# Graph attention and graph convolution on one core: four second-layer tiles a batch in halves by casting DMAs, the bias added by an accumulating DMA

## What is computed

```python
# first layer, per batch
h = input @ W;  f1 = h @ a1;  f2 = h @ a2
e = f1 + swapaxes(f2, 1, 2);  e = where(e >= 0, e, 0.2 * e)
attention = softmax(adj * e, axis=1)
x = attention @ h + bias + input
# second layer
support = x @ W1 + b
y = adj @ support
y = (y - mean) * rsqrt(var + 1e-5) * gamma + beta      # over batches and nodes
return relu(y) + x
```

## Time and profile before

| | |
|---|---|
| median of 3 runs | 909.66 us (909.13 to 911.93) |
| profiled execution | 911.96 us, its span 910.2 us |
| PE busy | 871.0 us, 96% |
| ACT busy | 804.2 us, 88% |
| DVE busy | 726.1 us, 80% |
| POOL busy | 211.6 us, 23% |
| moved by DMA | 246.39 MB, queue busy 71.7% |
| granted PE clock | 0.984 of full speed over the span, 1.00 in the batches |

### The profile page before, as it was taken

How to read it: one execution, slowest core, us unless ns; L and a number is a source line. 1 busy time by engine, 2 the same in 40 slices (tenths; PEclk the granted TensorE clock), 3 DMA queues, 4 the chain that set the end, 5 groups by cost and what they waited for, 6 DMA issues and landing times.

```text
span 910.2 us, 8919 instructions
## 1 busy us (share of the span) xinstructions
PE 871.0 (96%) x3167; PEld 547.5 (60%) x3167; DVE 726.1 (80%) x794; ACT 804.2 (88%) x614; POOL 211.6 (23%) x166
## 2 busy tenths in 40 slices
PE   6999999999999999999999999999999999999960
PEld 4335556675656756676566756567566765666850
DVE  3655788797878888887877978788888978879966
ACT  5998699988999799998999889997999979997645
POOL 0012214250333112341142401341113411323000
PEclk9999999999999999999999999999999999999995
DMA  8996676748677595867767495775957677565988
GB/s 337 422 362 240 260 291 237 292 165 334 224 273 268 203 360 173 294 234 267 280 237 300 155 357 207 267 274 199 358 174 292 231 263 287 192 224 190 423 335 344
DMA packets 46220, 246.39 MB, mean 271 GB/s; under 512 B 5560, under 2 KB 6184, under 8 KB 19552
## 3 DMA queue, kind: packets, MB, share of 16 engines
q1 hardware_dynamic: 46176, 245.82, 71.7%
HBM read 221.57 MB, written 24.23 MB: 270 GB/s over the span
## 4 chain that ended last, share of the span: by engine, by line
PE 83%; DVE 7%; ACT 3%; issue 2%; DMA 2%; SPq 1%; POOL 0%; DVEq 0%; ACTq 0%; POOLq 0%
PE acc L526 40%; PE acc L499 10%; PE acc L493 10%; PE acc L495 10%; DVE exp_lo L765 4%; PE acc L480 4%; PE acc L507 2%; PE acc L454 2%; PE acc L539 1%; PE acc L542 1%; PE acc L541 1%; ACT scores L623 1%; DMA adj_slot<-biasT 1%; DVE stats L786 1%; ACT hi L637 1%
## 5 line engine op out<-in xcount | busy, mean ns | idle before, releaser
L746 DVE CUSTOM_DVE_ANT_0 scores<-scores,adj_slot 128x2048 f32<-128x2048 f32 x128 | 297.5, 2324 | 77.5 <-ACT scores L616 30.2
L765 DVE SCALAR_TENSOR_TENSOR exp_lo<-scores,rz,hi 128x2048 fp32r<-128x2048 f32 (+1 forms) x133 | 280.5, 2125 | 0.0
L616 ACT ACTIVATE scores<-adj_slot,f_cols 128x2048 f32<-128x2048 f32 x128 | 255.0, 1998 | 15.4 <-PE acc L499 11.8
L623 ACT ACTIVATE scores<-scores,neg_mx 128x2048 f32<-128x2048 f32 x128 | 255.1, 1993 | 14.2 <-DVE neg_mx L749 14.2
L637 ACT ACTIVATE hi<-scores,rz 128x2048 fp32r<-128x2048 f32 (+1 forms) x133 | 227.5, 1726 | 33.6 <-DVE rz L758 30.4
L526 PE MATMUL acc<-adj_slot,region_even 128*128 128x512 f32 x512 | 228.8, 592 | 0.0
L526 PE MATMUL acc<-adj_slot,region_odd 128*128 128x512 f32 x392 | 175.3, 592 | 0.8 <-DVE region_odd L801 0.8
L526 PEld LDWEIGHTS acc<-adj_slot,region_even 128*128 128x128 f32 x512 | 96.7, 190 | 99.7 <-issue 95.7
L499 PE MATMUL acc<-exp_lo,h_hi 128*128 128x512 f32 x448 | 121.5, 391 | 0.8 <-DVE exp_lo L765 0.7
L526 PEld LDWEIGHTS acc<-adj_slot,region_odd 128*128 128x128 f32 x392 | 74.0, 190 | 77.2 <-issue 73.2
L495 PE MATMUL acc<-hi,h_hi 128*128 128x512 f32 x448 | 119.9, 390 | 0.0
(11 more groups left out here) (77 smaller groups left out, 614.7 us busy)
## 6 DMA issues: line engine op xcount, KB each, us to landing
adj_slot<-adjT SPq DMA_DIRECT2D x159, 1024.0 KB, 5.1
adj_slot<-xT SPq DMA_DIRECT2D x20, 1024.0 KB, 7.6
adj_slot<-biasT SPq DMA_DIRECT2D x32, 256.0 KB, 6.5
xp_dram<-adj_slot SPq DMA_DIRECT2D x32, 256.0 KB, 2.6
adj_slot<-xp_dram SPq DMA_DIRECT2D x8, 1024.0 KB, 12.1
adj_slot<-f_rows SPq DMA_DIRECT2D x7, 1024.0 KB, 6.9
adj_slot<-y_dram SPq DMA_DIRECT2D x7, 1024.0 KB, 12.0
outT<-adj_slot SPq DMA_DIRECT2D x6, 1024.0 KB, 4.7
```

What stands on the lines that cost most here:

```text
L616: act.activation(scores[t % ER][:, :], slots[f1_slot(bt.par)][:, :], ACT.Prelu, bias=f2_cols[:, bt.n, t:t + 1], alpha=ALPHA).then_inc(edge ...
L623: act.activation(scores[e][:, :], scores[e][:, :], ACT.Exp, bias=neg_mx[:, e:e + 1], accum_out=zsum[:, e:e + 1]).then_inc(exp_done, 1)
L746: dve.tensor_tensor_reduce(scores[e][:, :], scores[e][:, :], slots[s][:, :], 1.0, NEG_BIG, ALU.mult, ALU.max, mx[:, e:e + 1]).then_inc(max ...
L765: dve.scalar_tensor_tensor(exp_lo[e][:, part_cols(t, i)], scores[e][:, part_cols(t, i)], rz[:, e:e + 1], hi[m][:, part_cols(t, i)].bitcast ...
```

## The change

Three things change.

- **Halves for four tiles.** Places 3, 7, 10 and 14 of the second layer (tiles 5, 9, 12 and 0) are taken in halves, in batches 1 to 6; in batch 0 only places 10 and 14 (`FIRST_HI`). The hi half of the tile is loaded from DRAM once more by a DMA on POOL's queue whose destination is float32r, so that it rounds (`load_hi`), into a slot that is lent for it (`HI_AT`: the spare slot of tile 8, those of tiles 2 and 3, and that of tile 9). DVE makes the lo half in place (`tile_low`), in steps 1, 5, 8 and 11 (`LOW_STEP`). POOL splits the 128 columns of support that go with it (`split_support`), into one small buffer `part_hi`. PE takes 12 matmuls (`layer1_halves`).
- **The bias.** x is loaded a place earlier, and a DMA on POOL's queue adds the bias, reading biasT and accumulating into the slot of x. Its semaphore counts whole, so `make_xp` waits for all of it. Slot 9 no longer holds the bias.
- **Slots in turns.** In odd batches tiles 2, 3, 4 and tiles 9, 11, 10 swap slots (`SWAP`). The next batch's tiles 2, 3 and 4 are loaded at the end of the step before (`load_early`), around the store of x'. The adj tiles of lent slots are loaded again behind places 3 to 6 (`RELOAD`), into the slot that the second layer has left; tiles 2 and 3, lent now as well, behind places 7 and 10 (`LENT`), for the next step.

```diff
-    T_F, T_BIAS, T_X, T_RES = 8, 9, 10, 11
+    T_F, T_HI, T_X, T_RES = 8, 9, 10, 11
+    SWAP = {2: T_HI, 3: T_RES, 4: T_X}
+    SWAP.update({late: early for early, late in SWAP.items()})
+    HI_AT = {3: T_F, 7: 2, 10: 3, 14: T_HI}
+    LOW_STEP = {3: 1, 7: 5, 10: 8, 14: 11}
+    RELOAD = {T_F: 3, T_HI: 4, T_X: 5, T_RES: 6}
+    FIRST_HI = [10, 14]
+    LENT = {u: max(k for k in HI_AT if HI_AT[k] == u) for u in HI_AT.values() if u not in (T_F, T_HI)}
...
# SP
+            def load_early(nx, t):
+                wait_lent(nx.prev(), SWAP[t])
+                load_adj(nx, t)
+
+            def load_again(bt, t):
+                if t == T_F:
+                    sp.wait_ge(edge_out, NT * (bt.n + 1))
+                elif t in LENT:
+                    wait_l1(sp, bt.prev(), LENT[t])
+                elif not is_last(bt):
+                    wait_l1(sp, bt, SIGMA.index(SWAP[t]))
+                else:
+                    wait_lent(bt, t)
...
                     for k, t in enumerate(SIGMA):
                         wait_l1(sp, pv, k)
-                        if t >= PRE:
+                        if t >= PRE and k > 2:
                             load_adj(bt, t)
-                        elif not is_last(bt):
+                        elif t < PRE and not is_last(bt):
                             load_adj(nx, t)
-                        if k == 1:
-                            load_again(pv, T_F)
-                        if k == 2:
-                            load_again(pv, T_BIAS)
-                        if k == 3:
-                            load_again(pv, T_X)
+                        for t in RELOAD:
+                            if RELOAD[t] == k:
+                                load_again(pv, t)
+                        for t in LENT:
+                            if LENT[t] == k:
+                                load_again(bt, t)
-                        if k == T_BIAS + 1:
-                            load_bias(bt)
+                        if k == T_RES + 1:
+                            load_residual(bt)
-                        if k == 4:
-                            load_again(pv, T_RES)
-                        if k == T_RES + 2:
-                            load_residual(bt)
...
+                if not is_last(bt):
+                    load_early(nx, 2)
+                    load_early(nx, 3)
                 store_xp(bt)
+                if not is_last(bt):
+                    load_early(nx, 4)
...
# PE
+            def layer1_halves(bt, k):
+                t = SIGMA[k]
+                tile_hi = slots_lo[hi_slot(bt, k)]
+                pe.wait_ge(part_lo_done, split_no(bt, k))
+                pe.wait_ge(hi_loaded[k], hi_value(bt, k))
+                for c in range(NC):
+                    pe.matmul(acc1[c][:, :], part_lo[bt.par][:, tile_cols(t)], tile_hi[:, cols(c)], start=False, stop=False)
+                for c in range(NC):
+                    pe.matmul(acc1[c][:, :], part_hi[:, :], tile_hi[:, cols(c)], start=False, stop=False)
+                pe.wait_ge(tile_lo_done, split_no(bt, k))
+                for c in range(NC):
+                    mm = pe.matmul(acc1[c][:, :], part_hi[:, :], slots_lo[l1_slot(bt, t)][:, cols(c)],
+                                   start=False, stop=False)
+                mm.then_inc(l1_tile, 1)
...
# DVE
+                dve.wait_ge(hi_loaded[k], hi_value(bt, k))
+                dve.tensor_tensor(slots_lo[l1_slot(bt, t)][:, :], slots[l1_slot(bt, t)][:, :],
+                                  slots_lo[hi_slot(bt, k)][:, :].bitcast(F32), ALU.subtract).then_inc(tile_lo_done, 1)
...
-                dve.wait_ge(xb_done, NC * bt.n + c + 1)
+                dve.wait_ge(xb_done, 16 * (bt.n + 1))
...
+                    for k in (() if is_first(bt) else halved(bt.n - 1)):
+                        if LOW_STEP[k] == t:
+                            tile_low(bt.prev(), k)
...
# POOL
+            def load_hi(bt, k):
+                nx = bt.next()
+                if HI_AT[k] == T_F:
+                    pool.wait_ge(edge_out, NT * (bt.n + 1))
+                else:
+                    pool.wait_ge(max_done, NT * nx.n + HI_AT[k] + 1)
...
+                pool.dma_start(slots_lo[hi_slot(bt, k)][:, :], adjT[bt.n, tile_cols(SIGMA[k]), :])\
+                    .then_inc(hi_loaded[k], 16)
...
-            def add_bias(bt, c):
+            def add_bias(bt):
                 pool.wait_ge(res_loaded, 16 * (bt.n + 1))
-                pool.wait_ge(bias_loaded[c], 16 * (bt.n + 1))
-                pool.tensor_tensor(res_sb[:, cols(c)], res_sb[:, cols(c)], bias_sb[:, cols(c)], ALU.add)\
-                    .then_inc(xb_done, 1)
+                pool.dma_start(res_of(bt)[:, :], biasT, accum_op=ALU.add).then_inc(xb_done, 16)
...
-                    for b in range(NB):
-                        split_h(bt, b)
-                for c in range(NC):
-                    add_bias(bt, c)
+                    pv = bt.prev()
+                    split_h(bt, 0)
+                    halves_of(pv, 3, split_support)
+                    split_h(bt, 1)
+                    halves_of(pv, 7, load_hi)
+                    split_h(bt, 2)
+                    halves_of(pv, 10, load_hi)
+                    halves_of(pv, 7, split_support)
...
+                add_bias(bt)
+                if not is_last(bt):
+                    halves_of(bt, 3, load_hi)
```

More of the change, by code:

```diff
@@ L166, in build @@
         xn_loaded = sem("xn_loaded")
[L167 to L168 removed]
+        again_loaded = {t: sem(f"again_loaded{t}") for t in (T_F, T_HI, T_X, T_RES, *LENT)}
+        hi_loaded = {k: sem(f"hi_loaded{k}") for k in HI_AT}
+        part_hi_done, part_lo_done = sem("part_hi_done"), sem("part_lo_done")
+        tile_lo_done = sem("tile_lo_done")
         res_loaded = sem("res_loaded")
@@ L205, in adj_value, with again_value, hi_slot, split_no @@
                 return 16 * (bt.half + 1)
-            return 16 * (bt.n + 1 + (t in STAGED))
+            return 16 * (bt.n + 1 + (slot_of(bt.par, t) in STAGED))
         def l1_slot(bt, t):
-            if t == T_F and not is_last(bt):
+            if t in (T_F, T_HI, T_RES, T_X) and not is_last(bt):
                 return slot_of(1 - bt.par, t)
             return slot_of(bt.par, t)
+        def again_value(bt, t):
+            return 16 * (bt.n + (t not in LENT))
+        def hi_slot(bt, k):
+            if HI_AT[k] == T_F:
+                return l1_slot(bt, T_F)
+            return slot_of(1 - bt.par, HI_AT[k])
+        def split_no(bt, k):
+            return sum(len(halved(n)) for n in range(bt.n)) + halved(bt.n).index(k) + 1
+        def halved(n):
+            return FIRST_HI if n == 0 else list(HI_AT)
+        def hi_value(bt, k):
+            return 16 * (bt.n + (k in FIRST_HI))
         def part_cols(t, i):
@@ L561, in step @@
                         while ahead < min(t + (LEAD if t > 0 else LEAD - 1), NT):
-                            layer1(bt.prev(), ahead)
+                            if ahead in halved(bt.n - 1):
+                                layer1_halves(bt.prev(), ahead)
+                            else:
+                                layer1(bt.prev(), ahead)
                             ahead += 1
@@ L572, in step @@
                     for c in range(NC):
-                        make_h(nx, x1_sb if is_first(bt) else xn_sb, acc1, c)
+                        make_h(nx, x1_sb if is_first(bt) else xp_of(bt), acc1, c)
                 for c in range(NC):
@@ L642, in adj_high @@
                 t = SIGMA[LAST_SPLIT[m]]
-                if t in (T_BIAS, T_X, T_RES):
-                    act.wait_ge(again_loaded[t], 16 * (bt.n + 1))
+                if t in again_loaded and t != T_F:
+                    act.wait_ge(again_loaded[t], again_value(bt, t))
                 else:
@@ L758, in recip, with tile_low @@
                 dve.reciprocal(rz[:, e:e + 1], zsum[:, e:e + 1]).then_inc(rz_done, 1)
+            def tile_low(bt, k):
+                t = SIGMA[k]
+                if t in again_loaded and (bt.n > 0 or t not in LENT):
+                    dve.wait_ge(again_loaded[t], again_value(bt, t))
+                else:
+                    dve.wait_ge(slot_loaded[slot_of(bt.par, t)], adj_value(bt, t))
+                dve.wait_ge(hi_loaded[k], hi_value(bt, k))
+                dve.tensor_tensor(slots_lo[l1_slot(bt, t)][:, :], slots[l1_slot(bt, t)][:, :],
+                                  slots_lo[hi_slot(bt, k)][:, :].bitcast(F32), ALU.subtract).then_inc(tile_lo_done, 1)
             def exp_low(bt, t):
```

76 lines of the change are left out of this document (53 added, 23 removed).

## The result

The changed kernel takes 901.53 us (median of 6 runs, 901.14 to 905.20). The kernel before, measured beside it, takes 910.76 (909.13 to 911.95). The ratio is 0.9908 with a 95% interval of 0.9888 to 0.9928, so the change gives 9.2 us. 892.9 was predicted: the sign is right and the time is in the stated range (to 908), but only about half of the forecast gain of 16.8 came.

The account below looks back on a forecast made before the run. PE's matmuls were taken to bound the kernel, except at batch ends, where an ACT and DVE loop is as long. -17.9 + 1.4 - 2.3 + 2.0 = -16.8 us, from 909.66 to 892.9; range 888.5 to 908.

Parts of the forecast that it names:

- Halves, -17.9: Second layer on PE: 26 tiles taken in halves at 2.74 us instead of 3.43, saving 0.69 us each, -17.9 us.
- DVE, +1.4: DVE's added subtractions, 2.28 us each, delay scores and reciprocals; PE waits 0.2 us a batch, +1.4 us.
- Tail relief, -2.3: Batch ends: without POOL's bias additions two exp_lo run faster and the tail's 0.5 us wait goes in five batches, -2.3 us.
- Batch 0, +2.0: Batch 0: the accumulating DMA takes 7.5 us, so the bias sum is in at 92; +2.0 us, between -0.8 and +5.5.
- The step that failed: Batch end: x staged a tile sooner lands near 387, the sum is wanted near 403, leaving the bias DMA about 16 us.
- the sign of being wrong: Stated test of the forecast: it is wrong if PE waits over 1 us a batch or a casting load costs over 3.8 us.
- Their delay matters little: DMA queues: delay of the casting and accumulating transfers matters little, since a casting load goes out 20 to 35 us before use.
- B: Rival, chance 0.20: at batch ends ACT and DVE lag PE or collisions stay; PE waits 8.1 us in all, 901.
- C: Rival, chance 0.16: DMA queues bind, delaying tile loads and scores; decides from 3.8 us per special transfer; 925 at 4.25 us.
- D: Rival, chance 0.07: tile 9 lands too late for DVE in step 5; 2.5 us in each of seven batches, 910.
- The early loads: Next batch's tiles 2, 3 and 4 loaded early: no gain by itself, but puts ACT up with PE, covering the subtractions.
- the lower end that I took: DMA queues: a casting or accumulating transfer costs 2.83 us, like a plain one; the upper end was some 5.1 us.

## Why the prediction was right or wrong

**The sum, term by term.** The kernel with the residual x behind tile 15 differs from the changed kernel in one number, so it measures the terms without the lost batch ends. From the chains, in us from the span's start:

| kernel | second layer of batch 0 starts | first make_h after it | sixth make_h | span |
|---|---|---|---|---|
| before | 94.88 | 194.19 | 724.57 | 910.2 |
| bias alone | 98.53 | 197.19 | 726.12 | 911.2 |
| changed | 95.70 | 195.35 | 717.01 | 899.2 |
| x behind tile 15 | 96.58 | 193.80 | 708.27 | 890.5 |

- *Halves, -17.9.* Right. Steady batches with PE always busy last 105.78 without halves (the bias alone) and 102.90 with four: 2.88, or 0.72 a tile where 0.69 was forecast. 26 of them are 18.7 us.
- *DVE, +1.4.* Too much: PE waits for nothing in these batches. The subtraction takes 2.59 us on average in the changed kernel, where 2.3 was forecast, and DVE's 96 us of a batch still fitted. They fitted narrowly, as the run with 2.27 us more on DVE shows.
- *Tail relief, -2.3.* Right. In the kernel with the bias alone the steps of the table are shorter than before by 0.65, 1.45 and 0.55, together 2.65, and the two exp_lo take 4.6 where 4.7 was forecast. (Five batches at 0.5 would have been 2.5; 2.3 is two thirds of seven.)
- *Batch 0, +2.0.* +0.8 in the changed kernel, +1.7 and +3.65 in the two others, all inside the stated range. The accumulating DMA takes 8.34 us there, where 7.5 was taken. The transfers were thought of and the granted clock wasn't: where PE stood for 1.99 to 3.03 us, 1.6 us of the loss are the clock's. In the changed kernel PE happened to stand only 1.25. From trace to trace this start moves by up to 4.7 us with the same code, so one trace doesn't size the term.

-18.7 - 2.65 + 1.7 make -19.65, and the span with x behind is 890.5 against 910.2, -19.7. So the terms that were named hold; the missing 8.7 us (899.2 against 890.5) are one that wasn't. That the 892.26 of this kernel stands so near the forecast 892.9 is luck in part: its gain is 19.7 us and not 16.8, and the forecast was counted from 909.66, where the kernel before took 911.99 beside it.

**The step that failed** is on the bias: "x is staged a tile sooner and lands near 387 on that clock, and the sum isn't wanted until the first layer is over, near 403: the DMA has about 16 us. It gives something at the tail." The move of x was taken as room for the bias, and only the transfer that was moved was priced; what it does to tile 15 was put at nothing, without a reason. I did not ask what stands behind it on SP's queue, and that is tile 15, the one load at whose end everything waits. What it cost stands in the table: against the kernel with x behind, the changed one loses 2.4 us in the first step (99.65 against 97.22), 7.2 in the next five (521.66 against 514.47) and nothing in the last, and has 0.9 less in batch 0. That is 1.6 us a batch in six batches, over the 1 us that the forecast itself named as the sign of being wrong.

It shows as well in "Their delay matters little: a casting load goes out 20 to 35 us ahead of its use". It is true of the casting loads (their median is 5.5 us to landing and nobody waits), and it was the wrong transfer to look at: what a fuller queue delays is also every plain load, and the one of tile 15 has 5.2 us from its issue to the start of its score in the kernel before (385.32 to 390.5) and in the changed kernel only about 1 us to spare.

**The rivals.** *B*'s number, 901, was hit by the result, but not by its mechanism: the tail did bind, through a tile load and not through ACT and DVE being late. DVE's waits over the whole span of the changed kernel have this (line waited for: us in total, times, longest):

```profile
DVE scores L815 <- DMA adj_slot<-adjT: 25.2, 17, 4.0
```

In the kernel before such waits come to 20.4 us in 28 times, the longest 2.0.

*C* had the right place, "the load of a tile, which can't start until PE has freed its slot, with the score behind it on DVE", and the wrong measure. It asked whether the queues are full on average, and they weren't: 0.88 as forecast, and a casting MiB costs no more than a plain one. What counted was what stood ahead on the queue at the moment of issue. *D* did not come: with x behind tile 15 PE never waits, so tile 9 is in time.

**The early loads** were called "nothing by itself", a cover whose loss has B's price, 8.1 us. Right in kind: their loss costs 13.3.

**What the runs say of the queue's cost.** In the kernel with the bias alone the second queue holds nothing but the eight accumulating transfers:

```profile
q0 software_dynamic: 1152, 8.39, 4.9%
```

4.9% of its span of 911.2 us are 44.6 us, 5.6 for each MiB. The main queue (q1) of that kernel has 67.8%, 617.8 us, for 237.43 MB or 226.4 MiB, 2.73 each. So an accumulating MiB costs about twice a plain one. The prediction had weighed the rule of the Trainium skill (page "Collectives: The Full Stack", The bandwidth ceiling) that a reducing transfer runs at half rate; the trace agrees. In the changed kernel q0 holds 12.9% of 899.2, 116.0 us; less 44.6, if the eight accumulating ones cost the same here, it leaves 71.4 for 26 casting MiB, 2.75 each. Here the lower end that I took was right, and C's 3.8 was never near.

The issues on POOL were not held up by DVE:

```profile
L1002 POOL DMA_DIRECT2D adj_lo<-adjT x26 | 14.8, 571 | 112.7 <-DVE mx L815 97.7 <-ACT scores L685 15.0
```

571 ns on average over 26 issues leaves no room for waits of 2 us, while the casts on the same engine still show them (one of 128x128 took 2.35 us at 573.13 and another 0.29 at 618.54). This is as the Trainium skill has it ("SBUF — State Buffer", Who interferes with whom): two-input work on DVE holds only those of POOL's instructions that read SBUF.

## What to carry to other kernels

When a transfer is issued sooner, look at what now stands behind it on its queue, and price the load that an engine waits for at once, not only the one that was moved. Put a transfer that has time to spare behind one that has none; here that one number was worth 9 of the 20 us. And don't read spare room from a share: at 94% DVE and 89% DMA PE was always busy, and 2.3 us more on DVE in a batch made it 1.4 to 1.5 us longer. A run that is to add only traffic must be looked at in the queue's order too: the one here put its extra load ahead of the one that an engine waits for.

## What the runs showed of the hardware

- An accumulating DMA into SBUF takes the queues 5.6 us a MiB, a casting one 2.75, a plain one 2.73 (worked out above). From issue to landing the accumulating one takes 8.2 us (median, x behind tile 15) to 12.7 (the x of make_h behind), the casting one 5.5 in the changed kernel to 8.2 (without the early loads).
- Two MiB of x ahead of tile 15's load of 1 MiB, with the bias's transfer beside it, bring it from 5.1 us to 6.7 to 9.1; one MiB ahead of it can't be seen in the time (892.26 with one, 893.64 with none).
- PE's granted clock fell to 0.50 after waits of 1.99, 2.54 and 3.03 us in batch 0 and stayed at 1.00 after one of 1.25; the 16 float32 matmuls behind the wait took 5.47 us instead of 3.84.
- A wait can move along a chain of transfers with no gain: in batch 0 x landed sooner by some 3 us and the bias behind it took 2.6 us longer.
